# Moving layer 1's first product to the head of VectorE's step in a CIN + MLP kernel

## What is computed

```python
x0 = h = e                                            # (1024, 32, 64)
for i in range(2):
    z = einsum('bhd,bmd->bhmd', h, x0).reshape(batch, H * M, dim)
    out = relu(einsum('bcd,oc->bod', z, Ws[i]) + bs[i][None, :, None])     # 128 outputs
    if i == 0: h = out[:, :64, :]; finals.append(out[:, 64:, :])
    else:      finals.append(out)
z = sum(concatenate(finals, 1), -1)                   # (1024, 192)
h = relu(concatenate([z, dense_ctx], 1) @ W_top1 + b_top1)
h = relu(h @ W_top2 + b_top2)
y = h @ W_top3
```

## Time and profile before

| | |
|---|---|
| time, median of 3 runs | 1961.91 us (1961.3 to 1962.78) |
| the profiled execution | 1961.8 us |
| its span | 1960.0 us |
| PE (TensorE) busy | 1936.7 us, 99% of the span |
| DVE (VectorE) busy | 1913.6 us, 98% |
| POOL (GpSimd) busy | 1826.6 us, 93% |
| ACT (ScalarE) busy | 1729.8 us, 88% |
| the chain that ended last | PE 94% |
| granted TensorE clock | full in all slices |

### The profile page before, as it was taken

How to read it: one execution, slowest core, us unless ns; L and a number is a source line. 1 busy time by engine, 2 the same in 40 slices (tenths; PEclk the granted TensorE clock), 3 DMA queues, 4 the chain that set the end, 5 groups by cost and what they waited for, 6 DMA issues and landing times.

```text
span 1960.0 us, 28766 instructions
## 1 busy us (share of the span) xinstructions
PE 1936.7 (99%) x7258; PEld 1363.8 (70%) x7258; DVE 1913.6 (98%) x1246; ACT 1729.8 (88%) x1959; POOL 1826.6 (93%) x646
## 2 busy tenths in 40 slices
PE   6999999999999999999999999999999999999999
PEld 3677777767767777776776776777777677677676
DVE  6999999999999999999999999999999999999995
ACT  5889999989988998998998999899899899889986
POOL 5999999999999999999999999999999999999883
PEclk9999999999999999999999999999999999999999
DMA  8988877777777777777777777787787777777730
GB/s 227 244 202 196 198 181 195 197 182 193 194 186 188 196 189 185 195 193 181 196 193 181 194 194 187 189 199 188 181 197 195 182 194 193 185 190 196 186 93 1
DMA packets 277281, 364.27 MB, mean 186 GB/s; under 512 B 116353, under 2 KB 116737, under 8 KB 277138
## 3 DMA queue, kind: packets, MB, share of 16 engines
q1 hardware_dynamic: 265634, 352.01, 72.5%
q0 software_dynamic: 8192, 8.40, 1.9%
q10 hardware_dynamic: 3440, 3.68, 0.7%
HBM read 347.02 MB, written 16.78 MB: 186 GB/s over the span
## 4 chain that ended last, share of the span: by engine, by line
PE 94%; SPq 1%; DVE 1%; DMA 1%; issue 1%; POOL 0%; ACT 0%; DVEq 0%; ACTq 0%
PE out L823 22%; PE out L848 21%; PE out L842 21%; PE out L841 21%; PE out L831 7%; PE out L825 1%; DMA xrep<-fields_dram 0%; SPq L261 0%; PE hrep L898 0%; SPq L246 0%; DMA emb<-in_tables,ids_sb 0%; DMA fields_dram<-emb 0%; SPq L265 0%; DVE prod L734 0%; PE xr L898 0%
## 5 line engine op out<-in xcount | busy, mean ns | idle before, releaser
L319 POOL TENSOR_TENSOR zl<-prod,zh 128x2048 fp32r<-128x2048 f32 (+2 forms) x384 | 1581.9, 4152 | 26.5 <-ACT zh L483 24.8
L841 PE MATMUL out<-zh,w1h 128*128 128x512 f32 x1888 | 736.7, 390 | 1.4 <-ACT relu L489 1.4
L842 PE MATMUL out<-zh,w1l 128*128 128x512 f32 x1888 | 736.7, 390 | 0.0
L483 ACT ACTIVATE zh<-prod 128x2048 fp32r<-128x2048 f32 (+2 forms) x384 | 665.2, 1732 | 23.8 <-DVE prod L728 11.2
L496 ACT ACTIVATE hrep<-out,b_sb 32x512 f32<-32x512 f32 (+1 forms) x768 | 496.1, 646 | 127.8 <-PE out L825 117.8
L848 PE MATMUL out<-zl,w1h 128*128 128x512 f32 x1888 | 566.1, 418 | 1.6 <-POOL zl L319 1.6
L823 PE MATMUL out<-prod,w_sb 128*128 128x512 f32 x1024 | 460.1, 592 | 0.6 <-ACT relu L513 0.6
L848 PEld LDWEIGHTS out<-zl,w1h 128*128 128x128 f32 x1888 | 354.2, 188 | 130.9 <-issue 61.0
L841 PEld LDWEIGHTS out<-zh,w1h 128*128 128x128 f32 x1888 | 354.8, 188 | 104.3 <-issue 29.7
L842 PEld LDWEIGHTS out<-zh,w1l 128*128 128x128 f32 x1888 | 354.5, 188 | 76.3
L823 PEld LDWEIGHTS out<-prod,w_sb 128*128 128x128 f32 x1024 | 193.6, 189 | 195.7 <-issue 185.4
(11 more groups left out here) (71 smaller groups left out, 734.9 us busy)
## 6 DMA issues: line engine op xcount, KB each, us to landing
rot_high<-fields_dram SPq DMA_DIRECT2D x512, 256.0 KB, 4.2
rot_low<-fields_dram SPq DMA_DIRECT2D x508, 256.0 KB, 6.2
xrep<-fields_dram SPq DMA_DIRECT2D x252, 128.0 KB, 2.6
left_x<-fields_dram SPq DMA_DIRECT2D x254, 64.0 KB
left_y<-fields_dram SPq DMA_DIRECT2D x254, 64.0 KB
fields_dram<-emb SPq DMA_DIRECT2D x506, 32.0 KB, 4.6
emb<-in_tables,idx POOLq DMA_INDIRECT x244, 3.5
w_sb<-in_w SPq DMA_DIRECT2D x1, 1024.0 KB, 6.1
```

The costliest lines, as they stand in the source:

```text
L319: pool.tensor_tensor(zl[u][:, 0:size, :], product[:, 0:size, :], zh[u][:, 0:size, :].bitcast(F32), ALU.subtract).then_inc(zl_made[u], 1)
L483: act.activation(zh[u][:, 0:size, :], product[:, 0:size, :], ACT.Copy).then_inc(zh_made[u], 1)
L841: nc.tensor.matmul(out1[:, :], w1h[:, k, :], zh[u][:, t, :], start=start and t == 0, stop=False)
L842: nc.tensor.matmul(out1[:, :], w1l[:, k, :], zh[u][:, t, :], start=False, stop=False)
```

## The change

In VectorE's step, `prod1` (with its two waits) moves ahead of the layer-0 products of the next step, and these and the low part 4 of the step before move behind it. In odd steps `left_products` stands between them. Step 0 alone keeps its order. No instruction is added or removed, and the other engines' programs stay the same.

```diff
-                if is_up_to(i, c, LAST - 1):
-                    products_l0(m + 1, (c + 1) % 4, i + (c + 1) // 4 + 1)
-                if later:
-                    low_part4(m - 1, 1)
-                if b == 1 and is_up_to(i, c, LAST - 1):
-                    left_products(i * 2 + (c + 1) // 2)
+                if not later:
+                    products_l0(1, 1, 1)
                 dve.wait_ge(hrep0_made, m + 1)
                 if later:
                     dve.wait_ge(zl_made[0], m)
                 nc.vector.tensor_tensor(prod[1][:, :, :], repeated(hrep[0], LOW), low[:, :, :],
                                         ALU.mult).then_inc(p1_made, 1)
+                if b == 1 and is_up_to(i, c, LAST - 1):
+                    left_products(i * 2 + (c + 1) // 2)
+                if later and is_up_to(i, c, LAST - 1):
+                    products_l0(m + 1, (c + 1) % 4, i + (c + 1) // 4 + 1)
+                if later:
+                    low_part4(m - 1, 1)
                 if b == 1 and is_up_to(i, c, LAST - 1):
                     left_low(i * 2 + (c + 1) // 2)
```

## The result

The changed kernel takes **1966.22 us** (median of 11 executions, 1965.21 to 1967.47), the kernel before beside it 1961.65 (11 executions, 1961.3 to 1963.1). The ratio is 1.0023, with a 95% interval of 1.0015 to 1.0031: slower by about 4.6 us, where +1.4 was forecast. The time lies inside the stated range of 1961.2 to 1966.5, close to its upper end. The profiled execution of the changed kernel took 1966.22 us with a span of 1964.4, that is 4.4 over the span before, so the two profiled executions show nearly the whole difference.

The account below looks back on a forecast made before the run. TensorE was taken to bound the loop at 59.30 us for four steps. +1.54 us and -0.1 made +1.4 on 1961.8, 1963.2; the runs' median lies 0.1 higher, so 1963.3 us, range 1961.2 to 1966.5.

Parts of the forecast that it names:

- Rival 2: VectorE's head waits for `hrep0` and `zl0` in every step, mattering beyond 0.33 us per four steps: 15 us, 1978; chance 0.09.
- The stall of step 3: In the ramp TensorE waits 2.5 us for `zl4`, once; layer-0 matmuls start at 82.19 instead of 79.79.
- The delay is 1.54 us: Layer-0 matmuls of step 5 start at 111.75 instead of 110.21; a full TensorE never wins it back.
- I take no fall: TensorE's clock keeps its level through the 2.5 us wait in the ramp, adding no time.
- Rival 1: TensorE's clock falls in the ramp's stall, costing 2.4 us more: +3.8 us, 1965.7; chance 0.06.
- The covers: Later `prod0` (4.48 us even, 5.08 odd, behind VectorE's head) still precedes ScalarE's copy and TensorE's need.
- The waits for `hrep0` at heads from the teens on: VectorE, ahead of TensorE, would wait for `hrep0` at its heads from some step in the teens on.
- SP's queue: SP waits for `left_products`, said to come 0.5 us earlier; nothing moves in its DMA queue.
- The sum: +1.54 us in the ramp and -0.1 at the end make +1.4 us on the profiled execution.
- the end: In the last step an early `prod1` starts the chain of ScalarE and GpSimd 0.1 us sooner.

Follow-up runs that it names:

- e9: The changed kernel with the last tile of `prod1` as its own instruction between low part 4 and `z4` in even steps: 1963.91 us, ratio 1.0011.
- e4: The kernel before with low part 4 moved directly ahead of `z4` in even steps: 1964.38 us, ratio 1.0015.
- e5: The changed kernel with `left_low` moved behind the first half of `z4` in odd steps: 1977.92 us, ratio 1.0082.
- e10: The changed kernel, low part 4 ahead of layer-0 products in step 3 alone, `prod1`'s last tile between low part 4 and `z4` in even steps: 1963.87 us.
- e1: The changed kernel with low part 4 ahead of the layer-0 products in all steps: 1977.76 us, ratio 1.0085.
- e2: The changed kernel with low part 4 ahead of the layer-0 products in even steps only: 1980.7 us, ratio 1.0096.

## Why the prediction was off, step by step

The time fell into the range, near its upper end, and that is luck. It lies 2.9 us above the forecast. The range went up to 1966.5 to hold a fall of the clock, but some 2 of the 2.9 us came from the loop, which no term and no rival had.

- **"TensorE bounds the loop at 59.30 us for four steps, and VectorE alone would need 0.33 us less": right.** VectorE took over as the pace once 0.38 us were added to it, and the threshold lies between e9 (59.30, without the 0.38) and e4 (0.38 added, 59.35).
- **"Only times within VectorE's step move", "the steady loop stays at 59.30 us": this step failed.** VectorE's own need grew by 0.19 us in each even step, since low part 4 and the write of `z4` became neighbours. I had weighed each moved instruction against its readers on other engines, and never one VectorE instruction against the next. The window is 59.36, and it cost 1.8 us. The order's rows for step 2, printed above, show the new pair. Rival 2 named the right threshold, 0.33 us in four steps, and the wrong wait: it looked for it at the head, where VectorE waits for others.
- **The stall of step 3: right in place, length and cause.** 2.5 us between 77 and 80 forecast, 2.38 up to 79.06 measured. The forecast of 82.19 for the layer-0 matmuls missed by 1.06. The clock gave 1.54 (4.19 - 2.65); my 2.49 for two lows, six highs and three lows was 0.16 short of the 2.65 that they take at the full clock in e5; and the head of step 3 came 0.62 us sooner than assumed, since the DMA of `xrep` landed sooner (ScalarE's copy starts at 63.16, not 63.78). That head ranges from 72.8 to 74.4 us over the kernels that don't touch the start, as much as the terms that I summed to a tenth.
- **"The delay is 1.54 us": right as the price of the lag** (1.7 to 2.0 where the clock held). The stall isn't the cause of it but its form: taken from step 3, it came back in step 5 (e10).
- **"I take no fall" of the clock: wrong in the profiled execution and in 5 of the 11.** I had weighed the 2.5 us wait as nearer to one of 0.65 than to 16.94 us of idling; that was no ground. The sentence behind it, from the Trainium skill, that an idle array is put back to half its clock, was the better guide. Rival 1 had the mechanism, with a chance of 0.06 against 15 of 31 measured, and a price of 2.4 us taken from the start of the kernel; here it is 1.5, read directly, and 1.2 to 1.7 over two steps.
- **The covers.** Those of `prod0` held in the loop, though a little more lag breaks that of even steps (e1, e2). In step 3 ScalarE's copy did wait for the layer-0 products, 0.89 us up to 77.91, which is still earlier than the 78.80 of the kernel before. The head waited for `hrep0` once in the ramp, 1.09 us in step 4, because TensorE had fallen behind. The waits for `hrep0` at heads from the teens on didn't come (1.1 us over the whole kernel, in L712's group above), since VectorE sets the pace in the loop. But they don't come in e9 either, where TensorE does: between 130 and 1880 us its heads have no idle time, and the 3.1 us that VectorE idles stand ahead of its low parts (L683). So the head is not where a VectorE that is ahead waits, and rival 2 looked at the wrong place for this reason too.
- **SP's queue.** `left_products` comes 3.33 - 2.20 = 1.13 us earlier in an odd step, not 0.5 as I wrote. Nothing hangs on it.
- **The sum.** -0.62 for the earlier head, +3.28 for lag and clock, +1.79 for the loop: +4.45, against the 4.4 of the spans (the 0.1 that the end was to give back is within the rounding). By medians, each over the kernel before beside it, the changed kernel is at +4.6 and e9 at +2.4, so the loop's term is 2.1 and the ramp's 2.4. That fits 1.7 for the lag and 1.5 for a clock that falls in half of the executions (an estimate from the figures above).

**What stays open:** the exact share of the clock in the medians. e10 and e9 differ by 1.6 us from head to matmuls in their profiled executions, and by nothing in their medians (1963.87 and 1963.91). The six executions of e9 whose clock held have a median of 1962.94, 0.9 below e10's, so taking the stall out of step 3 may have a price of its own. The spreads overlap, and only one trace of each kernel shows where its head of step 3 stood.

## What to carry to other kernels

Where two engines are within about half a per cent of each other (here 0.33 us in 59.30), a reordering must be costed as the whole period of the engine that is *not* the bound, from start to start, with each new pair of neighbours looked at: does the second one wait for something the first one does? Put an independent instruction between them. And a consumer's distance behind a producer's head is a debt that is paid once, in the ramp, wherever TensorE can be made to give way; paid in one piece, it can cost the clock as well, here in about half of the executions.

## What the runs showed of the hardware

- The first half of `z4`, which waits on what its direct predecessor, a low part, signals, starts some 0.1 us after that one has ended, 1.31 to 1.32 us behind the start of an instruction of 1.21 to 1.22. An instruction without such a wait starts 0.08 us before that end, 1.13 behind. The difference is 0.19 us, in the changed kernel, in e4 and, by the windows, in e5. With a short instruction between them (e9) it is gone. The Trainium skill ("VectorE: DVE Perf Modes", section "The DRAIN you can't avoid") says of a chain of eight copies that a semaphore after each costs nothing extra. The trace here differs for its own instructions, and the measurement decides: where one waits on the one directly ahead, it costs 0.19 us.
- A wait of TensorE of 2.4 us was followed by a granted clock of 0.57 to 0.65 between 80 and 84 us in three profiled executions, and by a full one in a fourth. In the changed kernel two lows, six high matmuls and three lows behind it took 4.19 us, where the same took 2.65 at the full clock in e5.
- Over all executions of the four kernels with that wait, the mean granted clock shows a fall in 15 of 31. In the eight others tried, whose traces show no such wait over 1.2 us, it shows one in none of 77.
